# Second attention's bias sum and key vector: from the first pass to between the weight products at its end

## The reference

```python
# layer 0: three statistics of every score matrix, a network of two hidden layers, a temperature
scores = qk / math.sqrt(dk)
mean_sim = scores.mean(axis=(-2, -1))
max_sim = scores.max(axis=-1).mean(axis=-1)
probs = jax.nn.softmax(scores, axis=-1)
entropy_proxy = jnp.var(probs, axis=-1, ddof=1).mean(axis=-1)
feats = jnp.stack([mean_sim, max_sim, entropy_proxy], axis=-1)
hidden = gelu(_linear(feats, w1, b1)); hidden = gelu(_linear(hidden, w2, b2))
t = jnp.exp(jnp.clip(_linear(hidden, w3, b3), LOG_T_MIN, LOG_T_MAX))
# layer 1: queries, keys and values of 8 heads, all with biases
q = jnp.einsum('bld,hed->bhle', query, Wq) + bq[:, None, :]
k = jnp.einsum('bld,hed->bhle', key, Wk) + bk[:, None, :]
v = jnp.einsum('bld,hed->bhle', value, Wv) + bv[:, None, :]
...
return out @ Wc.T + bc
```

## Time and profile before

| | |
|---|---|
| median of 3 runs | 403.48 us (403.04 to 403.48) |
| profiled execution, its own time | 404.18 us |
| its span | 402.4 us |
| mean granted TensorE clock | 0.936 |
| PE busy | 349.9 us (87%) |
| DVE busy | 300.9 us (75%) |
| ACT busy | 278.7 us (69%) |
| POOL busy | 208.0 us (52%) |
| chain that ended last | PE 59%, DVE 18%, ACT 9%, issue 8% |

### The profile page before, as it was taken

One profiled execution on the slowest core, in us unless ns is written; L12 is line 12 of the kernel. 1 busy time (PEld: TensorE's weight loads), 2 busy tenths in 40 slices (PEclk: granted clock), 3 DMA queues, 4 the chain that ended last, 5 costly groups with the idle time before them and its releaser, 6 DMA issues.

```text
span 402.4 us, 12141 instructions
## 1 busy us (share of the span) xinstructions
PE 349.9 (87%) x4126; PEld 269.6 (67%) x4126; DVE 300.9 (75%) x1156; ACT 278.7 (69%) x834; POOL 208.0 (52%) x302
## 2 busy tenths in 40 slices
PE   2977788887589999976999999799999999878997
PEld 0523253455246767755899998668889989656886
DVE  5399998979537888998775444478898998885852
ACT  2499999979556778664577886458888888672340
POOL 3695778821102214777768800578888775432200
PEclk9999989869669999995999999979999999996999
DMA  7976639900000000112343331111101000000011
GB/s 228 334 216 188 192 109 315 384 2 2 1 4 5 5 6 18 37 48 77 109 120 84 98 93 55 33 39 37 29 23 29 23 23 3 2 2 1 22 34 52
DMA packets 36204, 31.00 MB, mean 77 GB/s; under 512 B 3504, under 2 KB 33584, under 8 KB 35504
## 3 DMA queue, kind: packets, MB, share of 16 engines
q1 hardware_dynamic: 33520, 24.98, 19.6%
q0 software_dynamic: 2048, 4.20, 3.6%
q10 hardware_dynamic: 576, 1.05, 0.8%
HBM read 14.94 MB, written 15.14 MB: 75 GB/s over the span
## 4 chain that ended last, share of the span: by engine, by line
PE 59%; DVE 18%; ACT 9%; issue 8%; DMA 2%; POOL 2%; POOLq 0%; DVEq 0%; SPq 0%; ACTq 0%
PE psum L1852 9%; PE psum L1802 6%; PE psum L1630 5%; ACT wa L690 5%; PE psum L1863 4%; PE psum L1785 4%; DVE scored L1164 4%; DVE scored L1151 3%; PE psum L1881 3%; PE psum L1670 3%; PE psum L1994 3%; PE psum L1904 2%; PE psum L1957 2%; PE psum L1920 2%; PE psum L1938 2%
## 5 line engine op out<-in xcount | busy, mean ns | idle before, releaser
L690 ACT ACTIVATE wa<-psum,scored 128x120 f32<-128x120 f32 x256 | 69.6, 445 | 5.8 <-DVE scored L1151 5.8
L1058 POOL DMA_INDIRECT c_area<-by_expert,rows_at x32 | 31.4, 981 | 34.2 <-DMA by_expert<-c_area 24.5
L1151 DVE TENSOR_REDUCE scored<-psum 128x8 f32<-128x960 f32 x32 | 36.7, 1146 | 11.9 <-PE psum L1670 11.8
L1164 DVE BATCH_NORM_STATS2 scored<-wa 128x6 f32<-128x240 f32 x128 | 43.3, 403 | 1.1 <-issue 0.3
L1852 PE MATMUL psum<-c_area,work 128*128 128x128 f32 x312 | 43.4, 284 | 0.1
L1670 PE MATMUL psum<-wa,qT 64*128 64x480 f32 x128 | 39.1, 695 | 2.5 <-ACT wa L690 2.5
L1852 PEld LDWEIGHTS psum<-c_area,work 128*128 128x128 f32 x312 | 39.5, 198 | 0.6 <-issue 0.4
L736 ACT ACTIVATE work<-psum 120x1024 f32<-120x1024 f32 x32 | 31.0, 1022 | 12.7 <-PE psum L1790 12.7
L970 POOL TENSOR_TENSOR rstd<-rstd,eps 128x2 f32<-128x2 f32 x16 | 12.6, 786 | 49.9 <-DVE rstd L1253 49.8
L926 POOL TENSOR_TENSOR wa<-kT,first 128x960 f32<-128x960 f32 x16 | 28.7, 1791 | 16.3 <-PE psum L1670 16.2
L1007 POOL DMA_INDIRECT by_expert<-scored,rows_at x32 | 31.5, 984 | 8.9 <-issue 8.9
(11 more groups left out here) (276 smaller groups left out, 1021.8 us busy)
## 6 DMA issues: line engine op xcount, KB each, us to landing
by_expert<-work SPq DMA_DIRECT2D x12, 768.0 KB, 7.6
c_area<-by_expert SPq DMA_DIRECT2D x39, 64.0 KB, 1.8
by_expert<-c_area SPq DMA_DIRECT2D x39, 64.0 KB, 1.6
upT<-in_up_dram SPq DMA_DIRECT2D x1, 2048.0 KB, 13.8
work<-in_heads_dram SPq DMA_DIRECT2D x1, 1536.0 KB, 8.9
late<-in_late_dram SPq DMA_DIRECT2D x1, 1098.0 KB, 10.4
x<-in_x_dram ACTq DMA_DIRECT2D x4, 256.0 KB, 5.6
ctxS<-in_ctx_classes_dram SPq DMA_DIRECT2D x1, 1024.0 KB, 10.1
```

Source lines behind the costliest of these rows:

```text
L690: e = nc.scalar.activation(prob[:, z, head, :], psum[:, score_bank(b, half) + h // 4, (h % 4) * LK:(h % 4 + 1) * LK], ACT.Exp, bias=rowneg ...
L1058: nc.gpsimd.indirect_dma_start(y_rows[:, r, j, :], None, by_expert[:, :], bass.IndirectOffsetOnAxis(rows_at[:, i:i + 1], 0)).then_inc(ld_y ...
L1151: nc.vector.tensor_reduce(rowneg[:, b * H0:(b + 1) * H0].rearrange("p (a c h) -> p a c h", a=2, c=2)[:, :, half], banks(score_bank(b, half ...
L1164: s = nc.vector.bn_stats(bnout[:, bass.ds(b * HALF0 + h // 2, 1), :].rearrange("p a s -> p (a s)"), prob[:, z, h:h + 2, :].rearrange("p h ...
```

## The change

The sums `bias1` and `uvec` leave the first pass. TensorE now makes them, in a new function `l1_sums`, between the second and the third group of weight products, into bank 0 (`uvec` first, then `bias1`). ScalarE copies them after the third product copy and before the last one. `wt_ps` counts them too, so product copies 2 and 3 wait for one more. The second pass's TensorE program waits, beside `wt_act` at 3, for `bias_act` at 3, that is for both copies, since its scores write bank 0. The temperature network's banks move: the second half's first layer from 0 to 5, the second layer from 5 to 1. TensorE's three waits for the end of queries, values and inputs now stand ahead of the products; what they wait for is long done by then.

```diff
--- before.py
+++ after.py
@@ -489,7 +489,7 @@
 
         CLIPPED, SCALED, COLUMNS, PARTS = ((2, 4), (5, 9), (7, 11), (8, 12))
         LAYERS, TURNED, WARM, HIGH = 3, 6, 4, 6
-        HIDDEN_BANKS = (4, 0)
+        HIDDEN_BANKS = (4, 5)
 
         def seqs_half(half):
             return slice(BH // 2 * half, BH // 2 * (half + 1))
@@ -602,7 +602,7 @@
 
         ROUTED = NB // 2
         DEVIATED = (slice(0, 14 * HALF0), slice(14 * HALF0, NB * HALF0))
-        BIAS_AT, BIAS1_AT, UVEC_AT = 4, 8, NB - 3
+        BIAS_AT = 4
         TURN_C, TURN_D, NORM_D, TAIL_D, LOGITS_D = 2, 2, 3, 4, 5
         GATHERS = 2
         LOGITS_B = 6
@@ -669,10 +669,6 @@
                 act.wait_ge(a_qps, b + 1)
                 if b == BIAS_AT + 2:
                     nc.scalar.copy(bias0[:, :], psum[:, 1, LQ:2 * LQ]).then_inc(bias_act, 1)
-                if b == BIAS1_AT + 2:
-                    nc.scalar.copy(bias1[:, :], psum[:, 1, LQ:2 * LQ]).then_inc(bias_act, 1)
-                if b == UVEC_AT + 2:
-                    nc.scalar.copy(uvec[:, :], psum[:, 1, LQ:LQ + H1]).then_inc(bias_act, 1)
                 nc.scalar.activation(qT[:, b, :], psum[:, 1, 0:LQ], ACT.Identity, bias=bq0,
                                      accum_out=qsum[:, b:b + 1]).then_inc(a_q, 1)
 
@@ -697,7 +693,7 @@
                               peel=NB)
 
             def product_copy(g):
-                act.wait_ge(wt_ps, g + 1)
+                act.wait_ge(wt_ps, g + 1 if g < 2 else g + 2)
                 nc.scalar.copy(product(g)[0], psum[:, PRODUCT_BANKS[g], :].rearrange("p (i d) -> p i d", d=D)).then_inc(wt_act, 1)
 
             act.wait_ge(a_dots, NB)
@@ -707,7 +703,7 @@
                 of = seqs_half(half)
                 for layer, bias in enumerate((b1c, b2c)):
                     act.wait_ge(mlp_pe, LAYERS * half + layer + 1)
-                    nc.scalar.activation(small[0:DH0, 6 + layer, of], psum[0:DH0, 5 if layer else HIDDEN_BANKS[half], of], ACT.Gelu, bias=bias[0:DH0]
+                    nc.scalar.activation(small[0:DH0, 6 + layer, of], psum[0:DH0, 1 if layer else HIDDEN_BANKS[half], of], ACT.Gelu, bias=bias[0:DH0]
                                          ).then_inc(mlp_act, 1)
                 if half == 0:
                     product_copy(0)
@@ -721,8 +717,12 @@
                 nc.scalar.copy(mparts[:, half, 0, :], psum[:, 5, half * P:(half + 1) * P]).then_inc(mlp_act, 1)
 
             high_parts(0)
-            for g in (2, 3, 1):
+            for g in (2, 3):
                 product_copy(g)
+            act.wait_ge(wt_ps, 3)
+            nc.scalar.copy(uvec[:, :], psum[:, 0, D:D + H1]).then_inc(bias_act, 1)
+            nc.scalar.copy(bias1[:, :], psum[:, 0, 0:D]).then_inc(bias_act, 1)
+            product_copy(1)
 
             def b_high_parts(b, z):
                 if b == 0:
@@ -1072,7 +1072,7 @@
 
             def d_add_bias(b, z):
                 if b == 0:
-                    pool.wait_ge(bias_act, 2)
+                    pool.wait_ge(bias_act, 3)
                 pool.wait_ge(tails["c"]["xn"], b + 1)
                 nc.gpsimd.tensor_tensor(x[:, b, :], x[:, b, :], bias1[:, :], ALU.add).then_inc(d_xb, 1)
 
@@ -1680,15 +1680,6 @@
                     pe.wait_ge(ld_heads, 64)
                     nc.tensor.matmul(psum[:, 1, LQ:2 * LQ], ones[0:1, :], bo0, start=True, stop=False)
                     nc.tensor.matmul(psum[:, 1, LQ:2 * LQ], bv0.to_broadcast([P, P]), w4T[:, 3, :], start=False, stop=True)
-                if b == BIAS1_AT:
-                    nc.tensor.matmul(psum[:, 1, LQ:2 * LQ], ones[0:1, :], bc1, start=True, stop=False)
-                    for h in range(H1):
-                        nc.tensor.matmul(psum[:, 1, LQ:2 * LQ], bqk1[:, 2, h:h + 1].to_broadcast([P, P]), wcT[:, h, :],
-                                         start=False, stop=(h == H1 - 1))
-                if b == UVEC_AT:
-                    pe.wait_ge(l1_folded, 5)
-                    for h in range(H1):
-                        nc.tensor.matmul(psum[:, 1, LQ + h:LQ + h + 1], l1N[:, 0, h, :], bqk1[:, 1, h:h + 1], start=True, stop=True)
                 nc.tensor.matmul(psum[0:LK, 1, 2 * LQ + H0 * b:2 * LQ + H0 * (b + 1)], kT[:, b, :], qmask[:, z, :], start=True, stop=True
                                  ).then_inc(a_dots, 1)
 
@@ -1702,12 +1693,23 @@
                 m.then_inc(wt_ps, 1)
 
             pe.wait_ge(l1_folded, 5)
-            for g in range(PRODUCTS):
-                pe.wait_ge(a_exp, 2 * NB - 2 + g // 2)
-                products(g)
+            def l1_sums():
+                for h in range(H1):
+                    nc.tensor.matmul(psum[:, 0, D + h:D + h + 1], l1N[:, 0, h, :], bqk1[:, 1, h:h + 1], start=True, stop=True)
+                nc.tensor.matmul(psum[:, 0, 0:D], ones[0:1, :], bc1, start=True, stop=False)
+                for h in range(H1):
+                    m = nc.tensor.matmul(psum[:, 0, 0:D], bqk1[:, 2, h:h + 1].to_broadcast([P, P]), wcT[:, h, :],
+                                         start=False, stop=(h == H1 - 1))
+                m.then_inc(wt_ps, 1)
+
             pe.wait_ge(a_q, NB)
             pe.wait_ge(a_v, X_GROUPS)
             pe.wait_ge(a_xc, NB)
+            for g in range(PRODUCTS):
+                pe.wait_ge(a_exp, 2 * NB - 2 + g // 2)
+                if g == 2:
+                    l1_sums()
+                products(g)
             pe.wait_ge(a_exp, 2 * NB)
             pe.wait_ge(w0_sb, 3)
             pe.wait_ge(a_neg, 2 * NB)
@@ -1725,7 +1727,7 @@
                     pe.wait_ge(f_dve, 4)
                 nc.tensor.matmul(psum[0:DH0, HIDDEN_BANKS[half], of], w1f[:, 2, :], small[:, 2, of], start=False, stop=True).then_inc(mlp_pe, 1)
                 pe.wait_ge(mlp_act, 2 * half + 1)
-                nc.tensor.matmul(psum[0:DH0, 5, of], w2T, small[0:DH0, 6, of], start=True, stop=True).then_inc(mlp_pe, 1)
+                nc.tensor.matmul(psum[0:DH0, 1, of], w2T, small[0:DH0, 6, of], start=True, stop=True).then_inc(mlp_pe, 1)
                 pe.wait_ge(mlp_act, 2 * half + 2)
                 nc.tensor.matmul(psum[:, HIDDEN_BANKS[half], BH + of.start:BH + of.stop], w3c, small[0:DH0, 7, of], start=True, stop=True
                                  ).then_inc(mlp_pe, 1)
@@ -1812,6 +1814,7 @@
                 nc.tensor.matmul(psum[:, 5, 0:D], oT[:, z, :], w4T[:, 3, :], start=True, stop=True).then_inc(b_y, 1)
 
             pe.wait_ge(wt_act, PRODUCTS - 1)
+            pe.wait_ge(bias_act, 3)
 
             def rank(r):
                 at, n = slots_of(r), 2 * BATCH_SEQS[r]
```

## The result

| | before | after |
|---|---|---|
| median in the rounds of the prediction | 403.48 us (403.04 to 403.64, 4 runs) | 408.32 us (407.48 to 409.66, 4 runs) |
| ratio | | 1.0088 (1.005 to 1.0126) |
| median in rounds of 12 runs (`a0_after` below) | 404.33 us | 408.22 us |
| ratio | | 1.006 (1.0027 to 1.0094) |
| profiled execution, its own time (span) | 404.18 us (402.4) | 407.97 us (406.2) |

The change makes the kernel slower, by 0.6 to 0.9% as ratios, 3.9 to 4.8 us in the medians. The direction was as forecast; 408.3 us lies above the predicted range. The ratio leaves out runs more than 1.5% above the same kernel's fastest, in the second pair the three highest of the changed kernel's 12 (410.01 to 410.30), which makes it the smaller number there.

A forecast was written before the change was run, and what follows sets the result against it. First pass bound by VectorE and ScalarE, with TensorE late behind the sums; then ScalarE's table load. Terms -3.6, +3.4, +1.7, +0.4 gave +1.9 us on 404.18; adjusted to run medians 405.4, stated 405.2 us, range 402.5 to 406.9.

The forecast's parts named there:

- First pass, -3.6 us: End of the first pass: removing bias1 gains 1.0 us and removing uvec 2.6 us, so it ends 3.6 us earlier.
- the lower bound for `uvec`: First pass, stall behind uvec: gain of 0 in an execution where TensorE has the full clock there.
- The block between the products, +3.4 us at the full clock: Sums between second and third product groups, ahead of the network: they and the products spend the first pass's gain, +3.4 us.
- The clock, +1.7 us: In the new block: one-column matmuls let TensorE fall to 1.2 GHz for one stretch, costing 1.7 us; chance 0.48.
- an earlier return of the clock: Second pass: it may get its full clock earlier, making the change cheaper; no separate size given.
- a smaller stall behind `uvec`: First pass: the stall may be smaller in other executions than profiled, making the change dearer; no separate size given.
- The copies, +0.4 us: Ahead of the second pass's first scores: two more ScalarE copies on the chain add 0.4 us, lower bound 0.
- The sum: Whole kernel: first pass -3.6, block +3.4, clock +1.7, copies +0.4, together +1.9 us against the profiled 404.18 us.
- The first pass gives little: Rival, first pass: gains 1.0 us or less while the block costs 3.4 to 5.1; 406.3 to 407.5 us; chance 0.13.
- The clock holds: Rival, new block: TensorE keeps 2.4 GHz, so +0.2 us, 403.7 us, no change; chance 0.24.
- The second pass starts warm: Rival, second pass: higher clock carries into its first sequences, 1.9 us come back, 401.8 us; chance 0.15.
- The rule weighed: New block: the skill blames idle gaps alone, so an unbroken stream keeps full rate and first Gelu comes at 100.8 us.

The follow-up runs named there:

- a0_after: The changed kernel itself, unaltered, timed again in the same rounds as other variants: 408.22 us, ratio 1.006 to the kernel before.
- e3: The changed kernel with neither sum made, uvec and bias1 filled by same-size copies from other tiles: 401.64 us, ratio 0.9938 to the kernel before.
- r2: The kernel before without bias1's nine matmuls, its copy taking ones, uvec still at sequence 13: 402.91 us, ratio 0.9977.
- e7: The changed kernel with both sums behind all four groups of products, not between the second and third: 405.02 us, ratio 1.0022 to the kernel before.
- e8: The changed kernel with ScalarE's two copies moved ahead of the temperature network: 406.99 us, ratio 1.0063 to the kernel before.
- e4: The changed kernel with uvec's eight matmuls 128 columns wide instead of one: 405.57 us, ratio 1.003 to the kernel before.
- e5: The kernel before with bias1 at sequence 9 instead of 8 and uvec's matmuls split over sequences 13, 14 and 15: 402.95 us, ratio 0.9982.

## Why the prediction was wrong

Two terms of the sum were mis-sized: the gain of the first pass, taken at 3.6 us and measured at 2.45 in the profiles, and the clock, taken at 1.7 us with nothing for what it does behind the block. In the profiles the mechanism of the rest came out as told.

*First pass, -3.6 us.* Right in kind, too large: without both sums the kernel is 2.6 us faster (`e3`, the copies still in it), and in the profile after the products start 2.45 us earlier. The price was read from one execution, in which the stall behind `uvec` was 2.75 us. In another it was 0.80 (`r2`). The profile after has a wait behind the group of values in place of the two, 1.17 us, that depends on the clock too. The prediction named the lower bound for `uvec` (0 at the full clock), but neither this case in its chance nor another late one in its sum.

*The block between the products, +3.4 us at the full clock.* Right: the kernel that in its profile has the sums at the higher clock (`e7`) is 3.4 us above that with none (405.02 for 401.64; both have the two copies). The chain goes where it was said to go, through the block to the first Gelu, for which ScalarE waits 5 us behind its table load.

*The clock, +1.7 us.* Right in the block, short behind it. The clock fell behind the one-column matmuls for a stretch as long as predicted, and the network started 7.68 us after the block's release (94.47 to 102.15) where the prediction's terms give 1.66 + 2.30 + 2.05 + 1.7 = 7.7; against `e7`'s 6.06 the fall cost 1.6 us. But between `e7` and the changed kernel lie 3.2 us in the medians and 1.5 in the ratios. By the medians, then, the term is too small by 1.5 us, by the ratios it is right. Part of the rest comes later: in the profile after the sparse stretch at 1.2 GHz reaches further into the second pass (L1804 3.26 us for 2.63 before), and behind the second pass's first scores another 1.25 us are lost against before (3.8 in span for 2.55). I had set an earlier return of the clock against a smaller stall behind `uvec` and let the two all but cancel (405.4 became 405.2 us); the clock went the other way, and the smaller stall was seen. In other executions the block itself is dearer, as in `a0_after`'s profile; how many of them are of that kind is open.

*The copies, +0.4 us.* Measured 0.25 in the chain (0.07 + 0.18) and 0.2 by `e8`. From the first Gelu to the first scores the profile after takes 7.52 us and that before 7.49, so hardly any of it is left over: the network was 0.2 us shorter.

*The sum.* By the medians -2.6 (copies in it) + 3.4 + 3.2 = +4.0 us, where the prediction had -3.6 + 0.4, + 3.4 and + 1.7. These three are differences along one row of kernels (before, `e3`, `e7`, changed), so that they add up to the measured +3.9 proves nothing; it shows how the miss is shared out, 0.6 us to the first pass and 1.5 to the clock. In the two profiles the shares are 1.15 us to the first pass and 1.25 to what follows the second pass's first scores, less 0.4 for the copies. Both errors pointed the same way. In the four runs of the prediction the changed kernel stood 4.8 us above before; the smaller set of runs of before was lower by 0.8 us than those of the later rounds.

*The rivals.* "The first pass gives little" held halfway (2.6 us, not 1.0). "The clock holds" is false in all profiles of this order and true in those of `e7` and `e4`. "The second pass starts warm" was false in all profiles: the scores of sequences 0 and 1 took 2.08 us in each.

*The rule weighed.* The loss of the full rate is laid to idle gaps by the Trainium skill, TensorE: Matmul & The Clock Gate, "HAM oscillation — how this bites in real kernels". The traces disagree: the profile after has TensorE at work without a gap from 94.47 to 103.5 us and at 1.2 GHz for 3.4 us of it, and `e7`, with the same idle gaps ahead (0.94 and 0.22 us), stays at 2.4 GHz, as does `e4` with 128 columns in place of one.

## What to carry to other kernels

A block moved off one engine's path has to be priced where it lands: here 4 us of matmuls left a place where they cost some 2.6 and came to one where nothing hid them. A run of one-column matmuls can cost more than its length: here the clock fell behind it where it followed 2.0 us of products and a short wait, and not where two more groups of products stood ahead. Behind the dense work the same sums were 3.2 us cheaper by the medians (1.5 by the ratios); splitting them was not proven to gain. A stall that ran at the lower clock in the one profile at hand has a second, smaller price; look for the clock before taking it whole.

## What the runs showed of the hardware that was not expected

Sixteen records of one column took 1.84 to 1.95 us at the higher clock (1.84 in `e7`, 1.92 in `r2`, 1.95 in the profile after; estimate before: 1.66) and 3.31 at the lower, against 2.05 for sixteen of 128 columns at the higher: with a 128x128 f32 weight load each, 127 more columns added 0.1 to 0.2 us to the sixteen. With one-column matmuls at work and no gap, the clock fell in one order (96.9 us in the profile after) and held in another (`e7`); and 3.31 us of them did not bring it back. The same kernel's executions differed by up to 6 us (401.2 to 407.5 for the kernel before). Where in the program the clock falls differs between profiles (in the first pass at 69.2 us in that of before, 69.7 after, 73.3 in `e5`). 12 runs of each left an interval of about 0.3% on either side.
